# Row maxima and exponentials of an attention over two PSUM banks at a time

## The chip, the cores and the metric

The kernel runs on one core of a Trainium2 chip. The metric is the device time of one execution, in microseconds. The engines are TensorE (PE, with its weight loads as PEld), VectorE (DVE), ScalarE (ACT), GpSimd (POOL) and SyncE (SP), which only issues DMAs. PSUM is where TensorE writes its results; the kernel lays it out in banks of 512 fp32 values per partition.

## What is computed

Two transformer layers over `x` of 4 x 256 tokens with 256 features, each a cross-attention and a feed-forward. The change is in the attention of the first layer:

```python
q = rms_norm(x_n @ Wq.T)                 # 16 heads of 128
kv_in = concat([context (1601), x_n (256)])
k = rms_norm(kv_in @ Wk.T); v = kv_in @ Wv.T   # 4 heads of 128, each for 4 query heads
q, k = rope(q), rope(k)
scores = einsum('bhqd,bhkd->bhqk', q, k) * SCALE
probs = softmax(scores)                  # over 1857 keys
attn = einsum('bhqk,bhkd->bhqd', probs, v)
return attn @ Wo.T
```

Then follow a mixture of experts, an attention over windows and a quantized feed-forward.

## The kernel before

`prepare` (some 180 us) normalizes and splits inputs, `attend` (until some 1375 us) is the attention above, `experts`, `window_attention` and `feed_forward` are the rest. Only `attend` is touched.

**Groups, tiles, slots.** `attend` runs 16 groups, one for each pair of a batch and a K/V head. The first two and the last two are written out, the other twelve are six passes of a loop with two groups in it. A group has 8 tiles (`TILES`): 128 queries of one head against all 1857 keys. A group has 8 slots, and all engines run through the same slots, each with its own program (`slot`, once per engine): slot i forms the scores of tile i and finishes tile i - 1. Into the slots the tasks of the next group are strewn by the table `SLOTS`: KV (projection of K and V, 8 of them), Q (2), KT and QT (transposes), and the current or last group's AT (transpose of the result) and WO (output projection). A task goes `ahead`, `amid` or `behind`. In slot 7 `ahead` is KT2, `amid` KT3 and `behind` nothing; in slot 5 they are AT0, KV7 and QT0; in slot 6 KT1, WO0 and QT1. The last group has no KV, Q, KT or QT to prepare; a tail of three slots finishes it.

**Precision.** Operands are split in two bf16 halves. Whatever TensorE leaves in PSUM, ScalarE copies to bf16 (high half), and VectorE writes what is left of it (low half). A product is three matmuls.

**PSUM.** The scores of a tile fill four banks (`scores`, `BANKS`: 512, 512, 512 and 321 keys). There is only one such set, so the next tile's scores overwrite these. Two banks hold transposed probabilities (`pT_ps`), one the output, one (`aux`) the tasks.

**One slot, by engine.** TensorE: `turn_probs` 0 and 1 of the old tile (L592: transposes, at most four blocks of 128 keys each), `form_scores` (L583: 12 matmuls), ahead, `apply_values` 0 (L604: 12 matmuls with V), `turn_probs` 2, `apply_values` 1, `turn_probs` 3, amid, `apply_values` 2 and 3 (12 and 9 matmuls), behind. VectorE: `probs_low` 0 and 1 (L845), `row_max` (L832, then `negmax` L834), ahead, `row_sum`, `probs_low` 2 and 3, then the squares for the norms of the K and Q rows projected in the slot before (`kjunk` L816, `qjunk` L825) and V's low half (L820), then the low halves of the tasks amid and behind (L807). ScalarE: `probs_high` 0 and 1 (L742), `output` (L754), V's high half, ahead, `probs_high` 2, exponential 0 (L748), `probs_high` 3, exponential 1, amid, exponentials 2 and 3, behind. GpSimd runs the rotation of the next group's K and Q (`rope`, L683 to L707); in it L692 waits for VectorE's squares.

**What waits for what.** Each engine works strictly in its order. Before, the row maximum of bank k waits for the scores of bank k; exponential 0 waits for `negmax`; the scores of bank k of the next tile wait for exponential k; `turn_probs` j waits for exponential j. `apply_values` j waits for `probs_low` j, which waits for `probs_high` j, which waits for `turn_probs` j. A task on TensorE waits until the one before it has left `aux`: WO after KT1 for `K`'s low half, KV7 after AT0 for `aT`'s.

Of the kernel before, what the change touches and what calls it, by code (L numbers as in the profile page):

```python
# [14 lines left out]
P = 128  # L15
# [6 lines left out]
NK = S + CTX  # L22
KT = -(-NK // P)
KP = KT * P
BANKS = [(k, min(512, NK - k)) for k in range(0, NK, 512)]
NB = len(BANKS)
PAIRS = (KT + 1) // 2
HALF = HD // 2
ROUND = 1.5 * 2 ** 23
# [58 lines left out]
def wait(eng, sem, value):  # L88

    if not isinstance(value, int) or value > 0:  # L90
        eng.wait_ge(sem, value)
# [330 lines left out]
def attend(nc, t, x, groups=GROUPS):  # L422
# [4 lines left out]
    with Scope(nc, "att") as sc:  # L427
# [19 lines left out]
        K = sc.sb("K", [P, 2, 2, KP], BF16)  # L447
        V = sc.sb("V", [P, 2, KT, 2, HD], BF16)
        Q = sc.sb("Q", [P, 2, 2, TILES, P], BF16)
        mx = sc.sb("mx", [P, 2, NB])  # L450
        negmax = sc.sb("negmax", [P, 4])
        es = sc.sb("es", [P, 4, NB])
        rsum, rinv = sc.sb("rsum", [P, 4]), sc.sb("rinv", [P, 4])
        prob = sc.sb("prob", [P, 2, KP])
        pT = sc.sb("pT", [P, 2, 2, KT, P], BF16)
# [12 lines left out]
        s = {n: sc.sem(n) for n in names}  # L468
# [5 lines left out]
        def nth(kind, n, g):  # L474

            return PER_GROUP[kind] * g + n + 1
# [20 lines left out]
        with nc.Block() as block:  # L497
# [27 lines left out]
            def _(pe):  # L525
# [48 lines left out]
                def form_scores(g, u, i):  # L574
                    tile = TILES * g + i
                    if i == 0:
                        pe.wait_ge(s["qt_lo"], nth("QT", 1, g))
                    for k, (lo, n) in enumerate(BANKS):
                        if i == 0:
                            pe.wait_ge(s["kt_lo"], nth("KT", k, g))  # L580
                        wait(pe, s["exp_done"], NB * (tile - 1) + k + 1)
                        for a, w in ((0, 0), (0, 1), (1, 0)):
                            last = nc.tensor.matmul(scores[:, lo:lo + n], Q[:, u, a, i, :], K[:, u, w, lo:lo + n],  # L583
                                                    start=(a, w) == (0, 0), stop=a == 1)
                        last.then_inc(s["qk_done"], 1)

                def turn_probs(tile, i, j):
                    wait(pe, s["exp_done"], NB * tile + j + 1)
                    wait(pe, s["pt_lo"], NB * tile + j - 1)
                    for m in range(quad(j)):  # L590
                        k0 = (4 * j + m) * P
                        last = nc.tensor.transpose(pT_ps[j % 2][:, m, :], prob[:, i % 2, k0:k0 + P], ident[:, :])  # L592
                    last.then_inc(s["pt_done"], 1)
# [116 lines left out]
            @block.scalar  # L710
            def _(act):
                def task(kind, n, ahead, g, u):
                    gt = g + ahead
                    par = (u + ahead) % 2
                    if kind == "WO":
                        return
                    act.wait_ge(s[DONE[kind]], nth(kind, n, gt))
                    if kind == "KV":
                        m = pair(n)
                        bank = aux[:, :].rearrange("p (m k) -> p m k", m=2)  # L720
                        wait(act, s["kp_done"], nth("KV", n, gt) - 4)
                        wait(act, s["v_lo"], nth("KV", n, gt) - 4)
                        nc.scalar.activation(kvraw[:, n % 4, 0:m, :], bank[:, 0:m, :], ACT.Copy).then_inc(s["kvraw_ready"], 1)  # L723
                    elif kind == "Q":
                        wait(act, s["qp_done"], nth("Q", n, gt - 1))
                        nc.scalar.activation(qraw[:, n, :, :].rearrange("p h d -> p (h d)"), aux[:, :], ACT.Copy).then_inc(s["qraw_ready"], 1)
                    else:
                        hi, _ = halves(kind, n, gt, par)
                        nc.scalar.activation(hi, aux[:, 0:hi.shape[-1]], ACT.Copy).then_inc(s[kind.lower() + "_hi"], 1)

                def values_high(kind, n, gt, par):
                    if kind == "KV":
                        m = pair(n)
                        if n == 0:
                            wait(act, s["pv_done"], TILES * (gt - 1))
                        act.wait_ge(s["kvraw_ready"], nth("KV", n, gt))
                        nc.scalar.activation(V[:, par, 2 * n:2 * n + m, 0, :], kvraw[:, n % 4, 0:m, HD:2 * HD], ACT.Copy).then_inc(s["vhi_ready"], 1)

                def probs_high(tile, i, j):
                    act.wait_ge(s["pt_done"], NB * tile + j + 1)  # L740
                    m = quad(j)
                    nc.scalar.activation(pT[:, i % 2, 0, 4 * j:4 * j + m, :], pT_ps[j % 2][:, 0:m, :], ACT.Copy).then_inc(s["pt_hi"], 1)  # L742

                def exponent(tile, i, k):
                    if k == 0:
                        act.wait_ge(s["negmax_ready"], tile + 1)
                    lo, n = BANKS[k]
                    nc.scalar.activation(prob[:, i % 2, lo:lo + n], scores[:, lo:lo + n], ACT.Exp, bias=negmax[:, i % 4:i % 4 + 1],  # L748
                                         scale=1.0, accum_out=es[:, i % 4, k:k + 1]).then_inc(s["exp_done"], 1)

                def output(tile, i):
                    act.wait_ge(s["pv_done"], tile + 1)
                    act.wait_ge(s["rinv_ready"], tile + 1)
                    nc.scalar.activation(attn[:, i, :], out_ps[:, i % 2, :], ACT.Copy, scale=rinv[:, i % 4:i % 4 + 1]).then_inc(s["o_done"], 1)  # L754

                def slot(i, g, u, first, prep, last):
                    ahead, amid, behind = (tasks_of(place, prep, first, last) for place in SLOTS[i])
                    tile, oi = TILES * g + i, (i - 1) % TILES
                    old = not (first and i == 0) and not (last and i > 0)
                    if old:  # L760
                        probs_high(tile - 1, oi, 0)
                        probs_high(tile - 1, oi, 1)
                    if not (first and i < 2) and not (last and i > 1):
                        output(tile - 2, (i - 2) % TILES)
                    for kind, n in projected(i, prep):
                        values_high(kind, n, g + 1, 1 - u)
                    for x_ in ahead:
                        task(*x_, g, u)
                    if old:
                        probs_high(tile - 1, oi, 2)  # L770
                    if not last:
                        exponent(tile, i, 0)
                    if old:
                        probs_high(tile - 1, oi, 3)
                    if not last:
                        exponent(tile, i, 1)
                    for x_ in amid:
                        task(*x_, g, u)
                    if not last:
                        exponent(tile, i, 2)  # L780
                        exponent(tile, i, 3)
                    for x_ in behind:
                        task(*x_, g, u)

                act.wait_ge(s["pad"], 4)
                for kind, n in FIRST_GROUP:
                    task(kind, n, 0, 0, 0)
                    values_high(kind, n, 0, 0)
                each_group(act, lambda g, u, first, prep: [slot(i, g, u, first, prep, False) for i in range(TILES)],
                           lambda g: [slot(i, g, 0, False, False, True) for i in range(3)])  # L790

            @block.vector
            def _(dve):
# [33 lines left out]
                        last.then_inc(s["q_ss"], 1)  # L827

                def row_max(tile, i):
                    for k, (lo, n) in enumerate(BANKS):  # L830
                        dve.wait_ge(s["qk_done"], NB * tile + k + 1)
                        nc.vector.reduce_max(mx[:, i % 2, k:k + 1], scores[:, lo:lo + n], AX.X).then_inc(s["bank_max"], 1)  # L832
                    dve.wait_ge(s["bank_max"], NB * tile + NB)
                    nc.vector.tensor_reduce(negmax[:, i % 4:i % 4 + 1], mx[:, i % 2, :], AX.X, ALU.max, negate=True).then_inc(s["negmax_ready"], 1)  # L834

                def row_sum(tile, i):
                    dve.wait_ge(s["exp_done"], NB * tile + NB)
                    nc.vector.reduce_sum(rsum[:, i % 4:i % 4 + 1], es[:, i % 4, :], AX.X).then_inc(s["sum_ready"], 1)
                    dve.wait_ge(s["sum_ready"], tile + 1)
                    nc.vector.reciprocal(rinv[:, i % 4:i % 4 + 1], rsum[:, i % 4:i % 4 + 1]).then_inc(s["rinv_ready"], 1)  # L840
# [1003 lines left out]
```

## Time and profile before

| | |
|---|---|
| median of 3 runs | 2259.17 us (2258.21 to 2295.41) |
| span of the profiled execution | 2254.6 us |
| PE busy | 1994.4 us, 88% of the span, 16352 matmuls |
| DVE busy | 1714.9 us, 76% |
| ACT busy | 1230.8 us, 55% |
| POOL busy | 1247.2 us, 55% |
| costly groups of the attention, busy | L604 (PE) 385.9 us, L583 (PE) 330.3 us, L748 (ACT) 329.8 us, L845 (DVE) 321.1 us, L832 (DVE) 292.1 us |

Busy time is the time in which an engine works on an instruction, those that only wait or issue DMAs left out. Instructions of one engine overlap at their ends, so their durations sum to more than the steps from start to start. A row of the timeline that says `x21` joins 21 instructions. In square brackets stands how long the engine was idle before the row, and which instruction ended it. The profile's chain of the work that ended last reaches back only through the last feed-forward, so it says nothing of the attention.

### The profile page before, as it was taken

What the parts mean: (1) busy time and instruction counts of PE and PEld (TensorE: products, weight loads), DVE (VectorE), ACT (ScalarE), POOL (GpSimd) and SP (SyncE); (2) the same over time, 40 slices, a digit from 0 to 9 for tenths busy, and PEclk for the clock granted to TensorE, in tenths of its full rate; (3) what the DMA queues carried; (4) which work ended last, traced back from release to release, by engine and by line L of the source; (5) the groups of instructions that cost most, each with busy time, mean ns of one, the idle gap of its engine ahead of it and who ended that gap; (6) DMA issues with size and microseconds to landing.
All of it is one profiled execution on the core that took longest, in us unless ns stands there. A gap on an engine that the chain in (4) does not pass through costs nothing. (4 is left out here: it accounts for less than half of the span.)

```text
span 2254.6 us, 49420 instructions
## 1 busy us (share of the span) xinstructions
PE 1994.4 (88%) x16352; PEld 1425.9 (63%) x16352; DVE 1714.9 (76%) x4116; ACT 1230.8 (55%) x2810; POOL 1247.2 (55%) x1724
## 2 busy tenths in 40 slices
PE   3438999999999999999999996899999999789897
PEld 3426877877777778778777775444444444338774
DVE  8756888778868787788688865699999999846435
ACT  2415676666666666667667663544444444363333
POOL 4424678657856676677567810466666666381110
PEclk8678999999999999999999997999999999896778
DMA  6761102210221022012201003122222222100000
GB/s 262 260 247 68 54 25 77 78 53 28 77 79 43 38 77 78 27 53 77 78 23 57 11 2 138 39 55 65 56 65 64 55 65 54 50 26 20 27 16 23
DMA packets 67176, 151.68 MB, mean 67 GB/s; under 512 B 26083, under 2 KB 36468, under 8 KB 63604
## 3 DMA queue, kind: packets, MB, share of 16 engines
q1 hardware_dynamic: 41236, 138.08, 16.7%
q0 software_dynamic: 22528, 5.35, 1.5%
q10 hardware_dynamic: 3168, 5.24, 0.6%
q8 instruction: 123, 2.02, 0.4%
q14 instruction: 121, 0.99, 0.1%
HBM read 121.94 MB, written 26.15 MB: 66 GB/s over the span
## 5 line engine op out<-in xcount | busy, mean ns | idle before, releaser
L845 DVE TENSOR_TENSOR att_pT<-att_pT 128x512 bf16<-128x512 f32 (+1 forms) x512 | 321.1, 651 | 196.4 <-ACT att_pT L742 193.5
L604 PE MATMUL att_out<-att_V,att_pT 128*128 128x128 bf16 x5760 | 385.9, 219 | 10.1 <-DVE att_pT L845 8.3
L742 ACT ACTIVATE att_pT<-att_pT 128x512 bf16<-128x512 f32 (+1 forms) x512 | 278.0, 571 | 199.1 <-PE att_pT L592 199.1
L604 PEld LDWEIGHTS att_out<-att_V,att_pT 128*128 128x128 bf16 x5760 | 350.1, 98 | 36.8 <-DVE att_pT L845 19.7
L748 ACT ACTIVATE att_prob<-att_scores,att_negmax 128x512 f32<-128x512 f32 (+1 forms) x512 | 329.8, 653 | 16.9 <-DVE att_negmax L834 15.8
L583 PE MATMUL att_scores<-att_K,att_Q 128*128 128x512 bf16 (+1 forms) x1536 | 330.3, 366 | 0.0
L832 DVE TENSOR_REDUCE att_mx<-att_scores 128x1 f32<-128x512 f32 (+1 forms) x512 | 292.1, 631 | 4.1 <-PE att_scores L583 3.9
L592 PE MATMUL att_pT<-att_ident,att_prob 128*128 128x128 f32 x1920 | 277.1, 275 | 16.8 <-issue 16.8
L1216 PE MATMUL moe_up<-rest_hhl,moe_up 128*128 128x512 bf16 (+1 forms) x1224 | 279.6, 383 | 8.0 <-POOL moe_up L1184 8.0
L1229 PE MATMUL moe_y<-moe_down,moe_hs 128*128 128x256 bf16 (+1 forms) x1632 | 242.4, 277 | 23.6 <-DVE all_x L1307 23.6
L1199 POOL DMA_INDIRECT moe_rows<-ktab_s,moe_turn x128 | 235.2, 1838 | 49.3 <-issue 49.3
L583 PEld LDWEIGHTS att_scores<-att_K,att_Q 128*128 128x128 bf16 x1536 | 152.8, 99 | 148.3 <-issue 9.8
L592 PEld LDWEIGHTS att_pT<-att_ident,att_prob 128*128 128x128 f32 x1920 | 210.7, 142 | 18.5 <-issue 17.7
L543 PE MATMUL att_aux<-att_wkv,att_kvT 128*128 128x256 bf16 x1440 | 179.9, 274 | 44.5 <-DMA att_kvT<-kv_s 21.1
L1216 PEld LDWEIGHTS moe_up<-rest_hhl,moe_up 128*128 128x128 bf16 (+1 forms) x1224 | 128.4, 109 | 143.0 <-issue 18.6
L1229 PEld LDWEIGHTS moe_y<-moe_down,moe_hs 128*128 128x128 bf16 (+1 forms) x1632 | 117.0, 96 | 154.2 <-issue 104.1
L683 POOL TENSOR_TENSOR att_scaled<-att_kvraw,att_kw 128x256 f32<-128x256 f32 x120 | 83.3, 694 | 197.0 <-ACT att_kvraw L723 197.0
L543 PEld LDWEIGHTS att_aux<-att_wkv,att_kvT 128*128 128x128 bf16 x1440 | 136.1, 98 | 67.0 <-DMA att_kvT<-kv_s 21.3
L1257 ACT ACTIVATE moe_silu<-moe_up 64x512 f32<-64x512 f32 (+1 forms) x204 | 113.8, 586 | 117.6 <-PE moe_up L1216 116.8
L1263 ACT ACTIVATE moe_hs<-moe_h 128x512 bf16<-128x512 f32 (+1 forms) x136 | 85.7, 630 | 168.7 <-DVE moe_h L1294 165.9
L1294 DVE TENSOR_TENSOR moe_h<-moe_up,moe_silu 64x512 f32<-64x512 f32 (+1 forms) x204 | 141.5, 693 | 35.5 <-ACT moe_silu L1257 16.9
L685 POOL TENSOR_TENSOR att_cosd<-att_scaled,att_tab 128x256 f32<-128x256 f32 (+2 forms) x150 | 125.1, 834 | 11.8
(247 smaller groups left out, 3395.7 us busy)
## 6 DMA issues: line engine op xcount, KB each, us to landing
att_kvT<-kv_s SPq DMA_DIRECT2D x16, 1920.0 KB
att_tab<-tab_s SPq DMA_DIRECT2D x16, 960.0 KB, 12.1
moe_up<-in_up_l SPq DMA_DIRECT2D x34, 368.0 KB, 3.2
moe_down<-in_down_l SPq DMA_DIRECT2D x34, 256.0 KB, 8.6
att_wq<-wq_s SPq DMA_DIRECT2D x16, 512.0 KB, 10.2
att_wo<-wo_s SPq DMA_DIRECT2D x16, 512.0 KB, 3.6
kv_s<-prep_kvhl SPq DMA_DIRECT2D x4, 1920.0 KB
prep_kv<-in_ctx_l SPq DMA_DIRECT2D x4, 1664.0 KB, 8.8
```

What stands on the lines that cost most here:

```text
L543: last = nc.tensor.matmul(o, kvT[:, par, a, c, k0:k0 + P], wkv[:, par, w, c, :], start=(c, a, w) == (0, 0, 0), stop=(c, a) == (DC - 1, 1))
L583: last = nc.tensor.matmul(scores[:, lo:lo + n], Q[:, u, a, i, :], K[:, u, w, lo:lo + n], start=(a, w) == (0, 0), stop=a == 1)
L592: last = nc.tensor.transpose(pT_ps[j % 2][:, m, :], prob[:, i % 2, k0:k0 + P], ident[:, :])
L604: last = nc.tensor.matmul(out_ps[:, i % 2, :], pT[:, i % 2, a, k, :], V[:, par, k, w, :], start=(k, a, w) == (0, 0, 0), stop=(k, a) == (KT ...
L742: nc.scalar.activation(pT[:, i % 2, 0, 4 * j:4 * j + m, :], pT_ps[j % 2][:, 0:m, :], ACT.Copy).then_inc(s["pt_hi"], 1)
L748: nc.scalar.activation(prob[:, i % 2, lo:lo + n], scores[:, lo:lo + n], ACT.Exp, bias=negmax[:, i % 4:i % 4 + 1], scale=1.0, accum_out=es[ ...
L832: nc.vector.reduce_max(mx[:, i % 2, k:k + 1], scores[:, lo:lo + n], AX.X).then_inc(s["bank_max"], 1)
L845: nc.vector.tensor_tensor(pT[:, i % 2, 1, 4 * j:4 * j + m, :], pT_ps[j % 2][:, 0:m, :], pT[:, i % 2, 0, 4 * j:4 * j + m, :], ALU.subtract) ...
L1199: pool.indirect_dma_start(out=rows[:, u, m, :], out_offset=None, in_=t["ktab_s"], in_offset=bass.IndirectOffsetOnAxis(ap=turn[:, u, m:m + ...
L1216: last = nc.tensor.matmul(o, up[:, u, w, c, c0:c0 + n], hhl[:, a, c, hf * SPAN:(hf + 1) * SPAN], start=(c, a, w) == (0, 0, 0), stop=(c, a) ...
L1229: last = nc.tensor.matmul(o, hs[0:n, hf, a, part, m * P:(m + 1) * P], down[0:n, u, w, part, :], start=(part, a, w) == (0, 0, 0), stop=(par ...
L1294: nc.vector.tensor_tensor(out, up_ps[3 * hf + k][64:64 + n, :], silu[64:64 + n, hf, k, :], ALU.mult).then_inc(s["h_done"], 1)
```

## The change

Exponential and row maximum take `SPANS` of two banks (1024 and 833 keys) in place of `BANKS`. A tile has two of each instead of four, and their partial results `mx` and `es` two columns. The counts of the semaphores follow: the first row maximum waits for the scores of two banks, the next tile's scores of a bank wait for the exponential over its pair of banks, `turn_probs` 0 and 1 wait for the first exponential, 2 and 3 for the second. On ScalarE the first exponential stands where exponential 0 stood, ahead of `probs_high` 3, and the second where 2 and 3 stood. Nothing else is moved.

```diff
+SPANS = [(k, min(1024, NK - k)) for k in range(0, NK, 1024)]
+NS = len(SPANS)
...
-        mx = sc.sb("mx", [P, 2, NB])
+        mx = sc.sb("mx", [P, 2, NS])
...
-        es = sc.sb("es", [P, 4, NB])
+        es = sc.sb("es", [P, 4, NS])
...
-                        wait(pe, s["exp_done"], NB * (tile - 1) + k + 1)
+                        wait(pe, s["exp_done"], NS * (tile - 1) + k // 2 + 1)
...
-                    wait(pe, s["exp_done"], NB * tile + j + 1)
+                    wait(pe, s["exp_done"], NS * tile + j // 2 + 1)
                     wait(pe, s["pt_lo"], NB * tile + j - 1)
...
-                    lo, n = BANKS[k]
+                    lo, n = SPANS[k]
...
                         exponent(tile, i, 0)
                     if old:
                         probs_high(tile - 1, oi, 3)
-                    if not last:
-                        exponent(tile, i, 1)
                     for x_ in amid:
                         task(*x_, g, u)
                     if not last:
-                        exponent(tile, i, 2)
-                        exponent(tile, i, 3)
+                        exponent(tile, i, 1)
...
                 def row_max(tile, i):
-                    for k, (lo, n) in enumerate(BANKS):
-                        dve.wait_ge(s["qk_done"], NB * tile + k + 1)
+                    for k, (lo, n) in enumerate(SPANS):
+                        dve.wait_ge(s["qk_done"], NB * tile + 2 * k + 2)
                         nc.vector.reduce_max(mx[:, i % 2, k:k + 1], scores[:, lo:lo + n], AX.X).then_inc(s["bank_max"], 1)
-                    dve.wait_ge(s["bank_max"], NB * tile + NB)
+                    dve.wait_ge(s["bank_max"], NS * tile + NS)
...
-                    dve.wait_ge(s["exp_done"], NB * tile + NB)
+                    dve.wait_ge(s["exp_done"], NS * tile + NS)
```

ScalarE's order in slot 7 of the second group, before: hi2 (L742, `att_pT` 128x512), exponential 0, hi3 (128x384), exponential 1, the transposed K of KT3, exponentials 2 and 3. A row is a line, an operation, its result and its operands.

```order
L729 ACTIVATE att_K<-att_aux 128x512
L742 ACTIVATE att_pT<-att_pT 128x512
L748 ACTIVATE att_prob,att_es<-att_scores,att_negmax 128x512
L742 ACTIVATE att_pT<-att_pT 128x384
L748 ACTIVATE att_prob,att_es<-att_scores,att_negmax 128x512
L729 ACTIVATE att_K<-att_aux 128x384
L748 ACTIVATE att_prob,att_es<-att_scores,att_negmax 128x512
L748 ACTIVATE att_prob,att_es<-att_scores,att_negmax 128x321
```

The same place in the changed kernel, whose lines stand two further on:

```order
L731 ACTIVATE att_K<-att_aux 128x512
L744 ACTIVATE att_pT<-att_pT 128x512
L750 ACTIVATE att_prob,att_es<-att_scores,att_negmax 128x1024
L744 ACTIVATE att_pT<-att_pT 128x384
L731 ACTIVATE att_K<-att_aux 128x384
L750 ACTIVATE att_prob,att_es<-att_scores,att_negmax 128x833
```

The copy hi3 (128x384) now stands behind an exponential over 1024 keys, and the copy of K behind hi3 at once.

VectorE's order in slot 4 of the second group, before: lo0 and lo1, four maxima, `negmax`, K's low half, the row sum, lo2 and lo3, the squares of Q.

```order
L845 TENSOR_TENSOR att_pT<-att_pT 128x512 x2
L832 TENSOR_REDUCE att_mx<-att_scores 128x1 x4
L834 TENSOR_REDUCE att_negmax<-att_mx 128x1
L807 TENSOR_TENSOR att_K<-att_aux,att_K 128x512
L838 TENSOR_REDUCE att_rsum<-att_es 128x1
L840 RECIPROCAL att_rinv<-att_rsum 128x1
L845 TENSOR_TENSOR att_pT<-att_pT 128x512
L845 TENSOR_TENSOR att_pT<-att_pT 128x384
```

And in the changed kernel:

```order
L844 TENSOR_TENSOR att_pT<-att_pT 128x512 x2
L831 TENSOR_REDUCE att_mx<-att_scores 128x1 x2
L833 TENSOR_REDUCE att_negmax<-att_mx 128x1
L806 TENSOR_TENSOR att_K<-att_aux,att_K 128x512
L837 TENSOR_REDUCE att_rsum<-att_es 128x1
L839 RECIPROCAL att_rinv<-att_rsum 128x1
L844 TENSOR_TENSOR att_pT<-att_pT 128x512
L844 TENSOR_TENSOR att_pT<-att_pT 128x384
```

Two maxima stand where four stood, and the rest keeps its place.

## Rows read from the trace of the kernel before

**Rows 1.** Table of stretches: 180 to 1375 us, almost all of the attention.

```profile
180.00:1375.00 1195.00, 1142.07 (x11596) 920.94 (x11595) 932.00 (x2373) 803.41 (x2059) 769.26 (x1350) 0.99 0.14 50
```

**Rows 2.** What TensorE waited for, 180 to 1375 us: total us, times, longest.

```profile
PE att_aux L543 <- DVE att_aT L807: 17.2, 15, 1.6
PE att_pT L592 <- issue: 16.8, 5, 3.5
PE att_out L604 <- DVE att_pT L845: 8.3, 23, 0.7
PE att_aux L570 <- DVE att_K L807: 4.1, 6, 0.7
```

**Rows 3.** Groups by line and shape, whole span: busy us, mean ns, idle before.

```profile
L748 ACT ACTIVATE att_prob<-att_scores,att_negmax 128x512 f32<-128x512 f32 x384 | 264.2, 690 | 16.9 <-DVE att_negmax L834 15.8
L748 ACT ACTIVATE att_prob<-att_scores,att_negmax 128x321 f32<-128x321 f32 x128 | 69.3, 541 | 0.0
L742 ACT ACTIVATE att_pT<-att_pT 128x512 bf16<-128x512 f32 x384 | 215.6, 599 | 198.7 <-PE att_pT L592 198.7
L1504 ACT ACTIVATE win_parts<-win_wqr 96x1024 bf16<-96x1024 f32 x1 | 1.0, 1041 | 0.0
L832 DVE TENSOR_REDUCE att_mx<-att_scores 128x1 f32<-128x512 f32 x384 | 241.0, 681 | 4.0 <-PE att_scores L583 3.9
L832 DVE TENSOR_REDUCE att_mx<-att_scores 128x1 f32<-128x321 f32 x128 | 61.6, 481 | 0.1
```

**Rows 4.** Timeline, a plain slot (group 10, slot 2): start us, us, engine, line.

```profile
956.88 0.60 ACT L742 ACTIVATE att_pT<-att_pT 128x512 bf16<-128x512 f32 x1 [2.25 <-PE att_pT L592]
957.38 0.68 ACT L748 ACTIVATE att_prob<-att_scores,att_negmax 128x512 f32<-128x512 f32 x1
958.04 0.49 ACT L742 ACTIVATE att_pT<-att_pT 128x384 bf16<-128x384 f32 x1
958.56 0.56 DVE L845 TENSOR_TENSOR att_pT<-att_pT 128x384 bf16<-128x384 f32 x1 [0.36 <-ACT att_pT L742]
958.98 1.34 PE L604 MATMUL att_out<-att_V,att_pT 128*128 128x128 bf16 x21
```

**Rows 5.** Timeline, slot 7 of group 10, the last row opens the next slot.

```profile
1002.47 2.27 DVE L832 TENSOR_REDUCE att_mx<-att_scores 128x1 f32<-128x512 f32 x4
1005.75 1.30 DVE L845 TENSOR_TENSOR att_pT<-att_pT 128x512 bf16<-128x512 f32 x2
1005.97 0.49 ACT L742 ACTIVATE att_pT<-att_pT 128x384 bf16<-128x384 f32 x1
1006.48 1.35 PE L604 MATMUL att_out<-att_V,att_pT 128*128 128x128 bf16 x21 [0.30 <-DVE att_pT L845]
1007.66 1.04 PE L592 MATMUL att_pT<-att_ident,att_prob 128*128 128x128 f32 x8
```

**Rows 6.** Timeline, slots 4 and 5 of group 10, then of group 11.

```profile
977.69 1.27 POOL L683 TENSOR_TENSOR att_scaled<-att_qraw,att_qw 128x512 f32<-128x512 f32 x1
977.71 1.39 DVE L825 SCALAR_TENSOR_TENSOR att_qjunk<-att_qraw 128x128 bf16<-128x128 f32 x1
987.80 0.39 PE L543 MATMUL att_aux<-att_wkv,att_kvT 128*128 128x256 bf16 x2 [1.62 <-DVE att_aT L807]
...
1051.32 0.56 DVE L845 TENSOR_TENSOR att_pT<-att_pT 128x384 bf16<-128x384 f32 x1 [0.17 <-ACT att_pT L742]
1051.79 0.28 DVE L825 SCALAR_TENSOR_TENSOR att_qjunk<-att_qraw 128x128 bf16<-128x128 f32 x1
1051.85 1.36 POOL L683 TENSOR_TENSOR att_scaled<-att_qraw,att_qw 128x512 f32<-128x512 f32 x1
1060.90 0.28 PE L543 MATMUL att_aux<-att_wkv,att_kvT 128*128 128x256 bf16 x1 [0.73 <-DVE att_aT L807]
```

**Rows 7.** Table of stretches: slot 0 of group 6, behind a loop's end.

```profile
628.70:640.84 12.14, 12.12 (x97) 9.11 (x97) 5.49 (x11) 5.55 (x14) 1.40 (x2) 0.75 0.01 3
```

**Rows 8.** Timeline, TensorE's weight loads ahead of PV3, slot 2 of the last group.

```profile
1328.67 0.51 PEld L604 LDWEIGHTS att_out<-att_V,att_pT 128*128 128x128 bf16 x9 [0.24 <-DVE att_pT L845]
```

## The prediction

> **What bounds the kernel now.** I first looked at the table of stretches, to see which engine limits the attention. The reader should see there that TensorE is busy 1142 of 1195 us [rows 1], so nothing that only shortens other engines can give much. Then the waits of TensorE over the same stretch: they name all it ever loses. 17.2 us go on `aT` (15 times, once per group that prepares another), 16.8 us on the loop's branches, 8.3 us on the low half of the transposed probabilities, 4.1 us on `K` [rows 2]. Together that is 46 us: it is all a gain can come from, and about 30 us of it hang on VectorE. The remaining question is how much cover each late result has, and this I read slot by slot from the timeline.
>
> I call the transposes of a tile's probabilities T0 to T3, their copies on ScalarE hi0 to hi3, their remainders on VectorE lo0 to lo3, and the products with V, PV0 to PV3. In a slot, TensorE does T0 T1 of the previous tile, the scores of this tile, PV0 T2 PV1 T3, then projections, then PV2 PV3. ScalarE does hi0 hi1, hi2, exponential 0, hi3, exponential 1, and so on.
>
> **Removed.** Per tile two maxima and two exponentials with their fixed cost.
> - VectorE: a maximum over 512 takes 681 ns and one over 321 takes 481 ns [rows 3], so 1.05 ns an element. Four of them take 2.27 us [rows 5]; take away the last one's 0.48 and three steps of 0.60 are left, of which 512 x 1.05 = 0.54 us are elements and 0.06 us are fixed. Two instructions fewer bring the maximum 0.12 to 0.13 us earlier.
> - ScalarE: the exponential's step to the next instruction, its accumulator's read included, is 957.38 to 958.04 = 0.66 us [rows 4]. The slope of the exponentials, (690 - 541) / 191 = 0.78 ns, gives 0.40 us for another 512 elements; that of the copies, (1041 - 599) / 512 = 0.86 ns, gives 0.44 us [rows 3]. I take 0.43, so a merged step is 1.09 us where two were 1.32. ScalarE gains 0.23 us for each, and is nowhere near full.
>
> **Added and moved.** hi3 stood behind a 512-wide exponential and now stands behind a 1024-wide one. It comes s = 0.43 us later, unless the exponential itself starts earlier. Does it? In a plain slot it starts 0.50 us after hi2 [rows 4], which is the step of one such copy: ScalarE is the limit there, and the earlier maximum changes nothing. It helps only where VectorE is late.
>
> Behind hi3 queue lo3 on VectorE, then the squares for the norms (`kjunk`, `qjunk`), and PV3 waits for lo3. So the slots differ by their cover:
> - Slots 1 to 4 and 6 have a projection ahead of PV2. In slot 2, lo3 ends at 958.56 + 0.56 = 959.12. The 21 products begin at 958.98 and take 0.056 us each (1006.48 to 1007.66 for 21, [rows 5]), so PV3, the last 9, begins at 959.65. Less some 0.06 us for the signal, the cover is 0.47 us against s = 0.43. It hides it, barely. Cost 0. Slot 0 is the same: its maxima are late by what the last exponentials before it take, and those end earlier now.
> - Slot 7 has only the short transposes of K there. hi3 moves from 1005.97 to 1006.40, ends 1006.89; lo3 runs 1006.92 to 1007.48; PV3 can begin at 1007.54, today at 1006.48 + 12 x 0.056 = 1007.15, where lo3's end at 1007.05 doesn't hold it [rows 5]. **+0.38 us, in 15 groups: +5.7.**
> - The last group prepares nothing, so nothing separates PV2 from T3, and PV3's weights wait for lo3 directly, 0.24 us [rows 8]. Six slots pay s and slot 0 about 0.16: **+2.7.**
> - Slot 5: KV7 waits for the low half of `aT`, which VectorE does behind the maxima. VectorE works without a pause from lo3 of slot 4 to there, and that lo3 waits for hi3 (0.17 us, <-ACT) [rows 6]. So the chain starts 0.43 later and its maxima give back 0.13: **+0.30 in 15 groups, +4.5;** in the seven odd ones lo3 then misses PV3 by another 0.08: **+0.6.**
> - Slot 6 of the six middle even groups waits for `K` behind maxima on a late VectorE: **-0.13 x 6 = -0.8** (4.1 us today, [rows 2]).
>
> The new waits of TensorE cost nothing. T0 needs both halves of the first exponential, done by 1006.5 in slot 7 where T0 starts at 1007.66 [rows 5]. The third bank's scores need the last exponential; they come behind T0, T1 (1.04 us, [rows 5]) and two other banks, and that exponential ends earlier than today. The first maximum needs two banks of scores; those are done before lo1 frees VectorE.
>
> Sum: 5.7 + 2.7 + 4.5 + 0.6 - 0.8 = +12.7 us on the profiled 2254.6 us, 2267.3. The median of the runs, 2259.17, lies 4.6 us above that span; the forecast is **2271.9 us**.
>
> One rule of the Trainium skill speaks for each side. Its page Perfetto Trace Analysis, section Optimizing Scalar/DVE Operations, says that larger operations help an engine that is saturated, and that on one that isn't, but makes bubbles on others, instructions should be broken up so that work is done sooner. ScalarE is busy 803 of 1195 us [rows 1]: by that rule the change goes the wrong way, which is what my terms say too. The same section gives about 125 ns of fixed cost for VectorE on PSUM, where the rows give 60; by it slot 5 would lose 0.18 instead of 0.30 us and the sum would be 10 us. The rows decide.
>
> **Rivals.**
> 1. *The phase between VectorE and GpSimd.* In slot 4 the first `qjunk` and GpSimd's multiplication (L683) start within 0.06 us of each other. Where VectorE is first it takes 0.28 us; where GpSimd is first it takes 1.39 us, as long as GpSimd's instruction lasts. TensorE's wait in slot 5 is then 1.62 us instead of 0.73 [rows 6], and slot 6 pays the wait for `K`, 4.1 / 6 = 0.7 us [rows 2]: 1.6 us a group. Six middle groups lose that race now, seven win it. Both sides move by s (GpSimd's chain waits for VectorE's squares in slot 3), so the race may fall either way: all lost +11 us, all won -10 us. I have it at zero, with 2283 and 2262 as its ends. The page SBUF — State Buffer of the Trainium skill (its rules on the shared port pair) says that such a pair excludes each other for a whole instruction; the row agrees, 1.39 us against 0.28. Chance that it falls badly by most of its size: 0.15; well: 0.15.
> 2. *hi3 isn't late by so much.* If the wide exponential cost less, say 0.2 us more than the narrow one, the terms would be 0.15, 0.2 and 0.07 us in place of 0.38, 0.43 and 0.3: about +4 us, 2263. Nothing in the rows speaks for it. 0.08.
> 3. *The fixed cost doesn't go away on ScalarE*, and s is 0.57 (two narrow instructions less one read). The covers of slots 1 to 4, 6 and 0 break by 0.05 to 0.1 us each, 0.4 us a group: with the larger slots 7 and 5, +10 on top, 2282. 0.12.
> 4. *Slower by over 2%.* That takes 45 us or 0.35 us in every one of 128 slots: s would have to be over 0.8 us, a read of two banks at half the rate. The 1024-wide copies show no such rate [rows 3], though they read another memory. Price at s = 1: 128 x 0.5 = 64 us, 2323. 0.05.
> 5. *It pays.* TensorE's waits behind VectorE's maxima shrink by 0.13 in slots 5 and 6 and hi3 is hidden after all: -4 us, 2255; with a lucky phase 2247. 0.05.
>
> A sixth thing moves under all of them: after a pass of the loop TensorE has been idle some 3.4 us (16.8 / 5, [rows 2]), and in the slot behind one of them it ran at 0.75 of its clock for 12.14 us [rows 7], about 0.25 x 12.14 = 3 us lost. There are five such places, worth 0 to 3 us each; I expect the same total, with some 4 us either way.
>
> **The numbers.** The main case, 2266 to 2278, has 0.40; the others as above, 0.15 + 0.15 + 0.08 + 0.12 + 0.05 + 0.05. The range goes from 2256 to 2288: it holds the main case and rivals 1 to 3, 0.90 together, each with the 4 us of the loop's ends; these carry some of rival 1 and 3 over its edges, and what is left out is between 1 and 2 in 10. A measurement of this kernel can tell about 2% (45 us) from no change. Only rival 4 is beyond that, and nothing reaches 2214: slower 0.05, faster 0.01, same 0.94.
>
> **What would show it.** In the profile after: exponential to hi3 1.09 us in a plain slot; four maxima's 2.27 us down to about 2.15; in slot 7 a new wait of TensorE for the low half of the probabilities between PV2 and PV3 of some 0.4 us, so that the 8.3 us of that wait become about 17; the wait for `aT` near 21 us; no wait of T0 or of the scores for an exponential. If slots 1 to 4 show waits ahead of PV3, s is larger than I think. If the wait for `aT` falls, the race with GpSimd has turned. If TensorE waits for an exponential, my reading of the new semaphore counts is wrong.

## The result, and the profile after

| | before | changed |
|---|---|---|
| median | 2258.71 us, 4 runs | 2277.03 us (2273.9 to 2278.38), 4 runs |
| ratio | | 1.0084, 95% interval 1.0066 to 1.0102 |
| span of the profiled execution | 2254.6 us | 2272.1 us |
| span of a second profiled execution | 2260.6 us | 2273.1 us |

The change costs 18.3 us by the medians (the ratio's interval gives 15 to 23), where 12.7 were forecast; the time lies in the forecast's main case. Now and then an execution of any variant takes some 40 us longer; the ratios leave such executions out, and so do the medians below that they would shift by more than 1 us.

First the table of stretches over the attention of the changed kernel, the answer to [rows 1]. The columns are start:end, length, then busy time and number of PE, PEld, DVE, ACT and POOL, the granted clock, the DMA share and GB/s.

```profile
180.00:1390.00 1210.00, 1137.60 (x11470) 922.59 (x11598) 917.74 (x2117) 742.13 (x1548) 770.52 (x1350) 0.99 0.13 50
```

ScalarE works 742 us in place of 803 and VectorE a little less, as meant, and TensorE still has its 1138: from the first T0 to the last PV3 the attention grew by 14 us (1180.2 to 1194.5) without any new work on it. The main waits of TensorE in that stretch, the answer to [rows 2] (us in total, times, longest):

```profile
PE att_out L606 <- DVE att_pT L844: 17.8, 53, 0.5
PE att_pT L594 <- issue: 17.3, 5, 3.8
PE att_aux L545 <- DVE att_aT L806: 16.5, 15, 1.2
PE att_aux L561 <- DVE all_x L802: 4.7, 8, 0.7
PE att_aux L572 <- issue: 1.4, 6, 0.3
```

The wait for the low half of the probabilities doubled (8.3 to 17.8 us). Taken apart by place: before, all of it stood ahead of PV2, and 7.2 us still do; new are 8.4 us ahead of PV3 (for lo3) and 2.3 us ahead of PV0 (for lo0), these in slot 5 of the eight even groups. The wait for `aT` did not grow in sum. The 4.1 us for `K` at WO (L570, now L572) are gone; 1.4 us that the profile puts down to "issue" stand there instead. And there is a wait that [rows 2] did not have and the prediction did not speak of: L561, the transpose of Q in slot 6, waits for `all_x` L802, VectorE's addition of WO's result. No wait for an exponential exists.

The groups by line and shape, over the whole span, answer [rows 3]:

```profile
L750 ACT ACTIVATE att_prob<-att_scores,att_negmax 128x1024 f32<-128x1024 f32 x128 | 142.1, 1110 | 15.6 <-DVE att_negmax L833 15.6
L831 DVE TENSOR_REDUCE att_mx<-att_scores 128x1 f32<-128x1024 f32 x128 | 155.2, 1213 | 6.7 <-PE att_scores L585 6.7
```

An exponential over 1024 keys takes 1110 ns where one over 512 took 690: 0.42 us more for twice the elements. Now the plain slot (group 10, slot 2), with columns as in [rows 4], which it answers:

```profile
966.58 1.11 ACT L750 ACTIVATE att_prob<-att_scores,att_negmax 128x1024 f32<-128x1024 f32 x1
967.67 0.49 ACT L744 ACTIVATE att_pT<-att_pT 128x384 bf16<-128x384 f32 x1
968.18 1.33 PE L606 MATMUL att_out<-att_V,att_pT 128*128 128x128 bf16 x21
968.19 0.56 DVE L844 TENSOR_TENSOR att_pT<-att_pT 128x384 bf16<-128x384 f32 x1 [0.79 <-ACT att_pT L744]
```

hi3 starts 966.58 to 967.67 = 1.09 us behind the exponential, so s = 1.09 - 0.66 = 0.43 us. lo3 ends at 968.75, PV3 can start at 968.18 + 12 x 0.056 = 968.85, and the 21 products stay joined: covered. Slot 7 of group 10 answers [rows 5]:

```profile
1011.36 2.14 DVE L831 TENSOR_REDUCE att_mx<-att_scores 128x1 f32<-128x1024 f32 x2
1015.27 0.84 PE L606 MATMUL att_out<-att_V,att_pT 128*128 128x128 bf16 x12 [0.28 <-DVE att_pT L844]
1015.29 0.49 ACT L744 ACTIVATE att_pT<-att_pT 128x384 bf16<-128x384 f32 x1
1015.81 0.56 DVE L844 TENSOR_TENSOR att_pT<-att_pT 128x384 bf16<-128x384 f32 x1 [0.59 <-ACT att_pT L744]
1016.42 0.68 PE L606 MATMUL att_out<-att_V,att_pT 128*128 128x128 bf16 x9 [0.31 <-DVE att_pT L844]
1016.94 1.04 PE L594 MATMUL att_pT<-att_ident,att_prob 128*128 128x128 f32 x8
```

Two maxima take 2.14 us, four took 2.27. The 21 products of [rows 5] are split now in 12 and 9, with a wait for lo3 between them; T0 starts 1016.94 - 1015.27 = 1.67 us behind PV2, and did 1.18. Slots 4 and 5 of the same group, the answer to the even half of [rows 6], and behind the dots the row of group 11:

```profile
987.33 1.27 POOL L685 TENSOR_TENSOR att_scaled<-att_qraw,att_qw 128x512 f32<-128x512 f32 x1
987.35 1.40 DVE L824 SCALAR_TENSOR_TENSOR att_qjunk<-att_qraw 128x128 bf16<-128x128 f32 x1
993.45 0.84 PE L606 MATMUL att_out<-att_V,att_pT 128*128 128x128 bf16 x12 [0.26 <-DVE att_pT L844]
996.94 0.83 PE L545 MATMUL att_aux<-att_wkv,att_kvT 128*128 128x256 bf16 x6 [1.20 <-DVE att_aT L806]
...
1070.42 0.83 PE L545 MATMUL att_aux<-att_wkv,att_kvT 128*128 128x256 bf16 x6 [1.01 <-DVE att_aT L806]
```

GpSimd is still first by 0.02 us in group 10, as it was. In group 11 the wait for `aT` grew from 0.73 to 1.01 us; in group 10 it fell from 1.62 to 1.20, as PV0 starts 0.34 us later into the slot (4.09 in place of 3.75) and KV7 0.06 us earlier (7.58 in place of 7.64). And the last group, the answer to [rows 8]:

```profile
1342.52 0.51 PEld L606 LDWEIGHTS att_out<-att_V,att_pT 128*128 128x128 bf16 x9 [0.67 <-DVE att_pT L844]
```

0.24 us have become 0.67: the difference is s, 0.43.

To put all this in one account, I measured in both traces each slot's length, from its T0 to the next, and took the difference.

| place | change per slot, us | sum, us |
|---|---|---|
| slots 0 to 4, but for the five slots 0 behind the loop | 0.00; slot 1 -0.04 to -0.08 | -0.7 |
| slot 5: odd groups and the two outermost (9) | +0.38 to +0.41 | +3.5 |
| slot 5: middle even groups (6) | 0.00 to -0.03 | -0.1 |
| slot 6: odd (7), outermost (2) | +0.50 to +0.53, +0.42 | +4.5 |
| slot 6: middle even (6) | -0.30 to -0.38 | -2.2 |
| slot 7, ten with no end of the loop behind | +0.38 to +0.42 | +4.0 |
| slot 7 at the loop's ends (5), slot 0 behind them (5) | -1.25 to +2.01 | +2.4, +0.2 |
| last group | six slots +0.42 to +0.43, slot 0 +0.17 | +2.7 |
| ahead of the first T0, behind the last PV3 | | +1.3, +2.0 |
| whole span (the rounded rows give 17.6) | | +17.5 |

### The profile page after: what moved, and what is told of

It reads as the page before. It is cut to its first block and busy times, and to the rows that moved or that the text cites. A ratio compares the mean times of both kernels' runs of the same rounds, so it can differ in the third digit from the quotient of the medians.

```text
span 2272.1 us, 48690 instructions
## 1 busy us (share of the span) xinstructions
PE 1998.3 (88%) x16186; PEld 1433.5 (63%) x16352; DVE 1700.6 (75%) x3860; ACT 1169.4 (51%) x2298; POOL 1249.8 (55%) x1724
## 5 line engine op out<-in xcount | busy, mean ns | idle before, releaser
L606 PE MATMUL att_out<-att_V,att_pT 128*128 128x128 bf16 x5760 | 389.3, 219 | 19.6 <-DVE att_pT L844 17.8
L585 PE MATMUL att_scores<-att_K,att_Q 128*128 128x512 bf16 (+1 forms) x1408 | 300.5, 362 | 7.7 <-issue 1.3
L1215 PE MATMUL moe_up<-rest_hhl,moe_up 128*128 128x512 bf16 (+1 forms) x1189 | 274.5, 383 | 11.8 <-POOL moe_up L1183 8.1
L831 DVE TENSOR_REDUCE att_mx<-att_scores 128x1 f32<-128x1024 f32 (+1 forms) x256 | 274.6, 1113 | 6.7 <-PE att_scores L585 6.7
L750 ACT ACTIVATE att_prob<-att_scores,att_negmax 128x1024 f32<-128x1024 f32 (+1 forms) x256 | 264.7, 1034 | 15.6 <-DVE att_negmax L833 15.6
L545 PE MATMUL att_aux<-att_wkv,att_kvT 128*128 128x256 bf16 x1440 | 187.8, 282 | 43.6 <-DMA att_kvT<-kv_s 20.4
```

What stands on the lines that cost most here:

```text
L545: last = nc.tensor.matmul(o, kvT[:, par, a, c, k0:k0 + P], wkv[:, par, w, c, :], start=(c, a, w) == (0, 0, 0), stop=(c, a) == (DC - 1, 1))
L606: last = nc.tensor.matmul(out_ps[:, i % 2, :], pT[:, i % 2, a, k, :], V[:, par, k, w, :], start=(k, a, w) == (0, 0, 0), stop=(k, a) == (KT ...
L1215: last = nc.tensor.matmul(o, up[:, u, w, c, c0:c0 + n], hhl[:, a, c, hf * SPAN:(hf + 1) * SPAN], start=(c, a, w) == (0, 0, 0), stop=(c, a) ...
```

## The experiments

**The change again, and the kernel before again.** These two say which differences between traces are the change's.

> The changed kernel once more, unaltered, for a second profile. What the theory of the late hi3 explains should repeat to 0.05 us a slot: TensorE +0.39 us in slot 7, +0.5 us in slot 6 of the odd groups, +2.7 us in the last group, 17.8 us of waits for the low half of the probabilities. What differs by chance should move: the time before the attention's first transposes (191.45 us before, 192.70 us after), the slots at the five loop ends, and the 2 us lost behind the attention.

> The kernel before once more, unaltered, for a second profile. The attention slot by slot as in the first, to 0.05 us, apart from the slots at the loop's ends. It is open whether the first profile was a short one outside the attention: behind the last product with V it took 881.7 us, and 882.7 to 885.7 us in the ten profiles of altered kernels; the first transposes came at 191.45 us, and at 191.1 to 193.8 us in those. If this one has some 884 us and 192.5 us, 2 to 3 us of the 17.5 us between the two profiled spans are chance; if it repeats 881.7 us and 191.45 us, they belong to the altered code.

The change again took 2274.92 us (one run; before, 11 runs beside it, 2258.05). The kernel before again took 2262.41 us, span 2260.6, 6.0 more than the first profile of the same program. All slots agree with the first trace of their kernel within 0.1 us, most within 0.03, but for the slots at the loop's ends. The slots of the two traces of before differ by 3.4 us in sum, all of it at the loop's ends; the part ahead of T0 by -0.4, the part behind the last PV3 by +3.0. The clearest case is slot 0 of group 10, once in each trace of the kernel before, in the table of stretches. First profile:

```profile
933.51:942.69 9.18, 9.18 (x96) 7.71 (x97) 5.14 (x11) 5.44 (x14) 1.40 (x2) 1.00 0.01 4
```

Second profile:

```profile
933.05:944.74 11.69, 11.47 (x96) 8.92 (x98) 5.48 (x11) 5.54 (x14) 1.40 (x2) 0.78 0.01 3
```

The same program and the same matmuls, once at a granted clock of 1.00 (2.4 GHz) throughout and once at 0.78 in the mean, behind the same idle time (3.25 and 3.21 us): 2.5 us. In the changed kernel the slot behind the loop that answers [rows 7] came at 0.84:

```profile
634.10:644.97 10.87, 10.65 (x96) 8.63 (x97) 5.21 (x9) 5.07 (x10) 1.40 (x2) 0.84 0.01 2
```

So the 17.5 us of the first pair of profiles hold several of chance. Over two profiles each, the spans differ by 2272.6 - 2257.6 = 15.0 us. What repeats is the slots, 11.7 us without the loop's ends; the slots 7 at the ends grew by 2.4 and 1.9 us in the two traces of the changed kernel against the first trace of before, about the 2.0 that five times 0.4 would be. That is 13.7 us located, of 18.3 measured with an interval from 15 to 23. The rest I can't assign.

**Only the maxima, or only the exponentials, on two banks.** All else is as before; for the first (the columns of `mx` follow):

```diff
-                    for k, (lo, n) in enumerate(BANKS):
-                        dve.wait_ge(s["qk_done"], NB * tile + k + 1)
+                    for k, (lo, n) in enumerate(SPANS):
+                        dve.wait_ge(s["qk_done"], NB * tile + 2 * k + 2)
```

> Only the row maxima work on two banks; the four exponentials stay. Theory of the late hi3: no cost is left, only the 0.13 us that VectorE gains, which reach TensorE in slot 5 of 15 groups and slot 6 of six: -2 to -4 us against before, about 2255 us. Rival, that reading two banks or waiting for two banks of scores costs by itself: 2259 us or more, and VectorE's maxima start later than 2.5 us into a slot.

> Only the exponentials work on two banks; the four row maxima stay. Theory of the late hi3: all of the loss and without VectorE's 0.13 us, so slots 5 and 6 lose some 0.13 us more in 15 groups: 2278 to 2282 us. Rival, that the pair of banks in the maxima is the cost: near 2259 us.

The wide maxima alone took 2248.24 and 2245.14 us (two more executions 2284.99 and 2285.82): the first two are 2246.7 in the mean against 2258.76 for before, 12 us **faster**, without an interval; the profiled span is 2246.5. The wide exponentials alone took 2275.99 us (median of three; two more 2314.26 and 2315.88), ratio 1.0078 (1.0055 to 1.0102), 2 us below the expected range. Its profile is that of the 2314.26 us, and all of its surplus lies behind the attention, so I read only the attention from it. The waits of TensorE with the maxima alone:

```profile
PE att_aux L545 <- DVE att_aT L809: 13.1, 15, 1.1
PE att_out L606 <- DVE att_pT L847: 5.5, 16, 0.5
```

and with the exponentials alone:

```profile
PE att_aux L545 <- DVE att_aT L806: 18.5, 15, 1.3
PE att_out L606 <- DVE att_pT L844: 16.8, 53, 0.5
PE att_aux L561 <- DVE all_x L802: 3.9, 7, 0.6
```

The whole loss is the exponentials', and I had expected a third of what the maxima bring. Per slot, against before, the maxima alone gave -0.10 (odd groups) and -0.45 (middle even ones) in slot 5, -0.34 and -0.75 in slot 6, where the instructions saved are worth 0.13. Most of the 0.34 is explained with the run of the addition below, and the 0.75 is not taken apart. The reason for 0.45 is in slot 5 of group 10 of the kernel before:

```profile
986.58 0.16 DVE L834 TENSOR_REDUCE att_negmax<-att_mx 128x1 f32<-128x4 f32 x1
987.05 0.69 DVE L807 TENSOR_TENSOR att_aT<-att_aux,att_aT 128x512 bf16<-128x512 f32 x1 [0.31 <-issue]
```

VectorE stood for 0.31 us ahead of `aT`'s low half and waited for nothing that the profile shows. In the changed kernel:

```profile
996.08 0.15 DVE L833 TENSOR_REDUCE att_negmax<-att_mx 128x1 f32<-128x2 f32 x1
996.19 0.69 DVE L806 TENSOR_TENSOR att_aT<-att_aux,att_aT 128x512 bf16<-128x512 f32 x1
```

The pause stands in six groups (1.9 us in sum) in every variant with both parts narrow, the kernel before again among them. With wide maxima alone it stands elsewhere, ahead of the low halves of the probabilities (1.7 us in 6), and with wide exponentials alone it is gone as well. So the length of a maximum doesn't decide it. In all the profiles, six to eight such pauses stand in every kernel with narrow exponentials, and in those with wide ones there is one at most; what it is I can't say. Maxima and pause are 0.13 + 0.31 = 0.44, the measured 0.45. With the exponentials alone, slot 5 of these groups grew by 0.09 to 0.12, which is s less the pause, 0.43 - 0.31 = 0.12.

**hi3 ahead of the first exponential.** If the loss is hi3's lateness, turning the two around removes it and keeps the saved instructions. The same edit was made to the changed kernel and to the one before:

```diff
-                    if not last:
-                        exponent(tile, i, 0)
                     if old:
                         probs_high(tile - 1, oi, 3)
+                    if not last:
+                        exponent(tile, i, 0)
```

> The changed kernel with hi3 ahead of the first exponential on ScalarE, nothing else. Theory of the late hi3: hi3 then starts when the transposes T3 are done, some 6.0 us into a slot in place of 6.56, and all of the loss goes; TensorE's wait in slot 7 between PV2 and PV3 is gone, and the maxima's 0.13 us are left: 2252 to 2258 us. The exponentials start 0.9 us later into the slot, which should cost nothing, since the next slot's T0 comes 7.8 us into it at the earliest. Rival, that wide exponentials or waits for pairs of banks cost by themselves: it stays above 2265 us.

> The kernel before with hi3 ahead of exponential 0. Theory: hi3 comes only 0.1 us earlier than before, because it then waits for T3; -0.5 to -2 us, 2257 to 2258 us. If it gains as much as the kernel with wide instructions and hi3 first, the order was the gain there, and not the fewer instructions.

The changed kernel with this order takes **2239.19 us** (2237.53 to 2243.23, 6 runs), ratio 0.9917 (0.9902 to 0.9932): 38 us less than the change as made, and 20 less than before, more than either theory had. Of the 14.7 us that the slots apart from the loop's ends lost against before, 11.5 are what the wide maxima bring alone. The waits of TensorE:

```profile
PE att_aux L545 <- DVE att_aT L806: 11.4, 15, 1.1
PE att_out L606 <- DVE att_pT L844: 5.7, 16, 0.7
```

17.8 + 16.5 + 4.7 us have become 5.7 + 11.4 and none. Slot 7 of group 10, to be set beside the one above: the products are joined again.

```profile
992.97 0.49 ACT L744 ACTIVATE att_pT<-att_pT 128x384 bf16<-128x384 f32 x1 [0.41 <-PE att_pT L594]
993.53 1.35 PE L606 MATMUL att_out<-att_V,att_pT 128*128 128x128 bf16 x21 [0.28 <-DVE att_pT L844]
```

In the kernel before the same edit **loses**: 2266.44 us, ratio 1.0039 (1.0027 to 1.0052), where I expected it level or 1 to 2 us faster. Its slots 0 and 2 to 4 are 0.10 to 0.12 us longer each (slot 1 by 0.02 to 0.10). Slot 2 of group 2 shows why:

```profile
353.79 1.33 PE L604 MATMUL att_out<-att_V,att_pT 128*128 128x128 bf16 x21
354.41 0.60 ACT L726 ACTIVATE att_qraw<-att_aux 128x512 f32<-128x512 f32 x1
355.06 1.48 PE L543 MATMUL att_aux<-att_wkv,att_kvT 128*128 128x256 bf16 x12
```

ScalarE copies the projection out of `aux` (L726) until 355.01, and only then may TensorE write the next one there. PV3 is done at 353.79 + 21 x 0.056 = 354.97, so the projection starts 0.09 late. With hi3 first, hi3 waits for T3 (ScalarE stands idle for 0.41 us ahead of it), and the exponentials and the copy come behind that. With two narrow exponentials ahead, 1.32 us, the copy comes too late; with one wide one, 1.09, it comes in time, in the same slot of the changed kernel with the new order:

```profile
350.41 1.34 PE L606 MATMUL att_out<-att_V,att_pT 128*128 128x128 bf16 x21
350.80 0.60 ACT L728 ACTIVATE att_qraw<-att_aux 128x512 f32<-128x512 f32 x1
351.59 1.47 PE L545 MATMUL att_aux<-att_wkv,att_kvT 128*128 128x256 bf16 x12
```

The copy starts 0.39 us behind PV2 and not 0.62, and the projection follows at 1.18 = 21 x 0.056. So here the 0.23 us that a merged exponential saves is worth something: not by itself, but because it lets hi3 go first.

**The order with only one part wide.** This asks whether both parts are needed.

> Maxima on two banks, four narrow exponentials, hi3 first. Theory: hi3 first pushes the two narrow exponentials and the copy out of aux behind them to 7.9 us into the slot, 0.1 us later than TensorE wants aux in slots 0 to 4; only wide exponentials save the 0.24 us that hide it. So it keeps the +0.1 us in some 70 slots: 2248 to 2252 us. Rival, that with hi3 first the width of the exponentials makes no difference: 2239 us, like the kernel with both.

> Exponentials on two banks, four narrow maxima, hi3 first. Theory: slots 0 to 4 are free of waits (the exponentials are short enough), but slots 5 and 6, which hang on VectorE, miss the 0.13 us of the maxima once or more each: 2243 to 2252 us. Rival, that the maxima bring nothing once the order is right: 2239 us.

Maxima alone, hi3 first: 2254.57 us (median of eight), ratio 0.9981 (0.9970 to 0.9992), above the 2248 to 2252 expected and far from the rival's 2239; its slots 0 and 2 to 4 are 0.10 to 0.12 us longer, as in the kernel before with that edit. Exponentials alone, hi3 first: 2246.66 us, 0.9945 (0.9927 to 0.9963), and no slot longer, the loop's ends apart. So hi3 first costs 8 us with narrow exponentials (2258.1 to 2266.4, and 2246.7 to 2254.6 with wide maxima) and brings 29 to 38 with wide ones (2276.0 to 2246.7, 2277.0 to 2239.2). For 2239 both parts are needed: without wide maxima it is 7.5 us more, without wide exponentials 15.4.

**The lateness without the width.** The kernel before, narrow, with hi3 behind both of its first two exponentials: s = 0.66 us, and the maxima as they were.

```diff
-                    if old:
-                        probs_high(tile - 1, oi, 3)
                     if not last:
                         exponent(tile, i, 1)
+                    if old:
+                        probs_high(tile - 1, oi, 3)
```

> The kernel before, four narrow exponentials and four maxima, but hi3 behind two exponentials in place of one: 0.66 us later, where the change makes it 0.43 us later. No instruction is wide. Theory of the late hi3: slot 7 +0.6 us, last group about +4.5 us, slot 6 +0.7 us in half of the groups, slot 5 +0.6 us, and the cover of 0.47 us in slots 1 to 4 breaks by 0.2 us each: +35 to +45 us, 2294 to 2304 us. Rival, that the width costs: 2259 us.

It takes 2305.57 us, ratio 1.0206 (1.0187 to 1.0225), 2 us above the expected range; span 2306.3. The waits are those from 180 to 1420 us, as this attention ends later:

```profile
PE att_out L604 <- DVE att_pT L845: 24.6, 68, 0.7
PE att_aux L543 <- DVE att_aT L807: 20.6, 15, 1.6
PE att_aux L570 <- DVE att_K L807: 10.4, 15, 0.8
```

Slot 7 grew by 0.63 to 0.67 us and six slots of the last group by 0.67, which is this s; the slots with a cover of 0.47, 0 and 2 to 4, grew by 0.19 to 0.21, where 0.66 - 0.47 = 0.19 (slot 1 by 0.11 to 0.19). Lateness alone makes this loss, and the cover that the prediction worked out for the plain slots is right to 0.02 us.

**WO's addition ahead of the squares.** To test the new wait in slot 6, VectorE does the tasks amid (the addition of WO's result among them) before the squares and V's low half:

```diff
+                    for x_ in amid:
+                        task(*x_, g, u)
                     for kind, n in projected(i, prep):
                         raw_rows(kind, n, g + 1, 1 - u)
-                    for x_ in amid + behind:
+                    for x_ in behind:
                         task(*x_, g, u)
```

> The changed kernel, with VectorE adding WO's result to x in slot 6 ahead of the squares of KV7 instead of behind them. The theory for the new wait in slot 6 (TensorE's QT1 waits for this add, 4.7 us in eight groups, and the add stands behind lo3 and the squares): QT1 no longer waits, slot 6 of the odd groups falls by 0.5 us or a little more, in all -5 us against the changed kernel: 2270 to 2273 us. Rival, that slot 6 is longer because GpSimd and VectorE collide differently: 2275 us or more, slot 6 stays near 9.56 us.

2264.09 us, ratio 1.0015 (1.0005 to 1.0026): 13 us less than the change as made, where 4 to 7 were expected. Its own profiled execution was 4 us above its median, and of the slots I can locate 7.4 us: odd slots 6 are 0.86 us shorter, 7 x 0.86 = 6.0, the outermost two 0.37, the middle even ones 0.11. Where the other 5 to 6 us went is open. The wait for `all_x` is gone. Why 0.86, and not the 0.52 that the change had added? Slot 6 of group 11 in the changed kernel:

```profile
1080.08 1.34 PE L606 MATMUL att_out<-att_V,att_pT 128*128 128x128 bf16 x21
1080.08 0.56 DVE L844 TENSOR_TENSOR att_pT<-att_pT 128x384 bf16<-128x384 f32 x1 [0.59 <-ACT att_pT L744]
1080.55 0.66 DVE L815 SCALAR_TENSOR_TENSOR att_kjunk<-att_kvraw 128x128 bf16<-128x128 f32 x1
1081.14 0.53 DVE L819 TENSOR_TENSOR att_V<-att_kvraw,att_V 128x128 bf16<-128x128 f32 x1
1081.59 0.41 DVE L802 TENSOR_TENSOR all_x<-att_aux,all_x 128x256 f32 x1
1082.06 0.66 PE L561 MATMUL att_aux<-att_ident,att_qp 128*128 128x128 f32 x4 [0.64 <-DVE all_x L802]
```

The chain is lo3, squares, V, addition, then TensorE. The same place in the kernel before:

```profile
1070.49 1.34 PE L604 MATMUL att_out<-att_V,att_pT 128*128 128x128 bf16 x21
1071.46 0.41 DVE L803 TENSOR_TENSOR all_x<-att_aux,all_x 128x256 f32 x1
1071.92 0.42 PEld L559 LDWEIGHTS att_aux<-att_ident,att_qp 128*128 128x128 f32 x4 [0.27 <-DVE all_x L803]
1071.93 0.66 PE L559 MATMUL att_aux<-att_ident,att_qp 128*128 128x128 f32 x4
```

PV3 ends at 1070.49 + 1.18 = 1071.67, the addition at 1071.87, the transpose starts at 1071.93. TensorE waited there before, too. The matmul's row shows no idle time, since the modelled end of the products lies past it; the weight load's row has it. From PV2 to the transpose it was 1.44 us, and became 1.98, where 1.18 are work: 0.80 of the 0.86 are these two waits. With the wide maxima alone it is 1.17 us in the same place: the old wait is gone there too, which is 0.27 of that variant's 0.34.

**Both orders together.**

> The changed kernel with hi3 ahead of the first exponential and the add of slot 6 ahead of the squares. If QT1 still waits for the add in slot 6 there, it gains up to 3 us more on the kernel with hi3 first (2236 to 2239 us); if hi3 first has freed it already, no difference, or a little loss where the squares, now later, hold up the next slot.

2240.46 us, ratio 0.9919 (0.9904 to 0.9935): the same as hi3 first alone. Slot 6 of the odd groups is 0.86 us shorter than in the change as made with either edit, and with both still 0.86: with hi3 in time the addition is in time as well, so both edits mend the same lateness. In the even groups the addition's edit takes off another 0.1 us each, under 1 us in all.

## Why the prediction was right, and where its steps were not

- **The plain slots: right.** s is 0.43 us, in slots 0 to 4 of all groups but the last nothing is added, and slot 1 even gains a little (0.7 us in sum, which was not forecast), and the narrow variant with s = 0.66 confirmed the cover of 0.47.
- **Slot 7: right**, +0.40 against 0.38; fifteen of them make about 6 us against 5.7.
- **The last group: right**, 2.7 against 2.7.
- **Slot 5: right in nine groups, wrong in the six middle even ones.** 0.39 came where 0.30 + 0.08 stood for the odd ones, and 0.40 where 0.30 stood for the outermost two, but -0.02 where +0.30 stood. The step that failed is "the chain starts 0.43 later and its maxima give back 0.13": the chain held a pause of 0.31 us, which vanished. The total is 3.4 us against 5.1. That the wait for `aT` would be near 21 us fell with it (16.5). In the odd groups it did grow by 0.29; in the even ones a part of the lateness showed up ahead of PV0 instead, 2.3 us in sum, and the pause was gone. It did not fall because the race with GpSimd had turned, which was my sign for it: the squares lose it still.
- **That the waits in [rows 2] name all that TensorE loses: wrong.** The one of 0.27 us ahead of the transpose of Q in slot 6 was hidden behind the modelled end of the matmuls, and it is part of what the next step missed.
- **Slot 6: wrong.** The step was its listing with slots 1 to 4: "It hides it, barely. Cost 0." I asked for lo3 only whether PV3 waits for it. Behind lo3 stand the squares, V and WO's addition, and for that the next task on `aux` waits: +0.50 us in nine slots (4.5). In the middle even groups the gain was 0.37 and not 0.13. The total is +2.3 us against -0.8.
- **The new waits cost nothing: right.** TensorE never waits for an exponential, and VectorE's maxima wait for scores only in slots 0 (6.7 us in sum in place of 3.9).
- **The sum: in part luck.** Located is 13.7 us against 12.7, but as errors of -1.7 (slot 5), +3.1 (slot 6), -0.7 (slot 1) and +0.3 (slot 7) that nearly cancel. Measured is 18.3; no slot that repeats holds the other 4.6. The sixth thing, the loop's ends, had been given 4 us either way, but that it took them is not shown.
- **The rivals.** 1, the race: it did not turn. 2 and 3, another s: no, 0.43. 4: no, though s = 0.66 in the narrow variant reached 1.0206. 5, that it pays: only with the other order. The Trainium skill (Perfetto Trace Analysis, Optimizing Scalar/DVE Operations) says that on an engine that isn't saturated but causes bubbles on others, breaking up instructions may let work be done sooner. The wide exponentials as made agree with that, 1.0084 for the change and 1.0078 for them alone; the order with 0.9917 does not, as the same wide exponentials are the faster ones there (2239.2 us against 2254.6 with narrow ones). What decides here is which instruction stands behind which.

## What to carry to other kernels

Fewer, wider instructions on an engine that isn't the bound can pay or cost: here the wide maxima alone took off 12 us, as TensorE waits for what VectorE does behind them, and the wide exponentials alone added 17. Look for the short instruction queued behind the wide one, for which the bounding engine waits, and put it first. Then see whether the time saved by merging is what makes that order possible: here the order lost 8 us in the kernel before, and in the changed one it turned the loss of 18 into a gain of 20. When a result gets later, follow all that its engine does behind it until the next thing another engine waits for, and look for hidden waits in the weight loads' rows as well as in the matmuls'.

## What the runs showed of the hardware

- One instruction of ScalarE or VectorE over two PSUM banks runs at about the rate of one bank: the exponential takes 690 ns for 512 and 1110 for 1024 elements, the maximum 681 and 1213. Merging saves 0.23 us a pair on ScalarE (its accumulator's read among it), and 0.06 to 0.07 us a pair on VectorE.
- VectorE had pauses of 0.31 us that end with "issue", in the same place of six groups. They moved when only the maxima were made wide, and were gone when only the exponentials were, which is another engine's code. Their sum was 1.9 us, as much as some terms of the forecast.
- Behind the same idle time the same slot came once at a granted clock of 1.00 in 9.18 us and once at 0.78 in 11.69. The two variants with both parts wide and hi3 first, 2237.3 and 2237.7 us in the profile, both came through two of the five such slots in 9.19 us, and the other kernels through one or none. Whether this belongs to their order, and is part of the 38 us that it brings over the change as made, is open: the slots apart from the loop's ends explain 26.5 of them.
